# Local attention on Trainium2: where the softmax's division is done

## What is computed

```python
def local_attention(q, k, v):              # 8 heads of 64, windows of 128 tokens
    bq = q.reshape(b, h, w, WINDOW, d) * QK_SCALE
    bk, bv = (look_around(bk), look_around(bv))   # the window before and the own one: 256 keys
    sim = jnp.einsum('bhwid,bhwjd->bhwij', bq, bk)
    mask = (i < j) | (i > j + WINDOW) | (j == -1)
    sim = jnp.where(mask, -jnp.finfo(sim.dtype).max, sim)
    attn = jax.nn.softmax(sim, axis=-1)
    out = jnp.einsum('bhwij,bhwjd->bhwid', attn, bv)

def _layer(x, wqkv, qs, ksc, wo, ...):
    qkv = shift_token(x) @ wqkv
    q = l2norm(q) * qs; k = l2norm(k) * ksc
    q, k = rotary_xpos(q, k)
    x = x + local_attention(q, k, v) @ wo
    ...                                     # then a gated feed-forward
```

## Time and profile before

| | |
|---|---|
| median of 3 runs | 3619.47 us (3614.95 to 3624.1) |
| the profiled execution, its own time | 3632.49 us |
| its span, first to last instruction | 3630.7 us |
| mean granted TensorE clock over the span | 0.947 |
| local attention, layer 0, first to last score matmul | about 772 to 1241 us of the span |
| local attention, layer 1 | about 1537 to 2001 us |
| TensorE busy over the whole span | 3202.5 us (88%) |
| VectorE busy | 2445.3 us (67%) |
| ScalarE busy | 1847.3 us (51%) |

### The profile page before, as it was taken

One profiled execution on the slowest core, in us unless ns is written; L12 is line 12 of the kernel. 1 busy time (PEld: TensorE's weight loads), 2 busy tenths in 40 slices (PEclk: granted clock), 3 DMA queues, 4 the chain that ended last, 5 costly groups with the idle time before them and its releaser, 6 DMA issues. The chain is left out here.

```text
span 3630.7 us, 52188 instructions
## 1 busy us (share of the span) xinstructions
PE 3202.5 (88%) x18048; PEld 1973.5 (54%) x18048; DVE 2445.3 (67%) x4613; ACT 1847.3 (51%) x3942; POOL 1410.3 (39%) x968
## 2 busy tenths in 40 slices
PE   8499999979999799899999899798388888887867
PEld 5244444346666555566666555333255555555756
DVE  8488887657777622277777332498599999997623
ACT  2177776846666421166666211365377777774100
POOL 4201111132222211132222211243599999996522
PEclk9699999989999899999999999899699999999888
DMA  5945666110020043000200121343525151512874
GB/s 171 157 58 89 85 91 125 34 35 23 23 65 23 26 156 97 26 23 23 65 23 19 55 70 47 97 159 141 222 77 204 58 204 58 203 58 73 280 232 153
DMA packets 276034, 347.27 MB, mean 96 GB/s; under 512 B 70619, under 2 KB 207817, under 8 KB 275132
## 3 DMA queue, kind: packets, MB, share of 16 engines
q1 hardware_dynamic: 261860, 308.29, 30.7%
q10 hardware_dynamic: 9432, 23.35, 2.0%
q0 software_dynamic: 4480, 12.30, 0.9%
HBM read 227.72 MB, written 112.80 MB: 94 GB/s over the span
## 5 line engine op out<-in xcount | busy, mean ns | idle before, releaser
L2373 POOL TENSOR_TENSOR H_feed<-H_ndu,H_bs 128x1024 f32<-128x1024 f32 x256 | 595.2, 2369 | 6.6 <-DMA H_cs<-between_bc 4.0
L888 ACT ACTIVATE B_probs<-B_p_exp,B_key_bias 128x512 f32<-128x512 f32 (+3 forms) x768 | 394.7, 582 | 168.0 <-PE B_p_exp L950 137.1
L779 DVE TENSOR_REDUCE B_part_max<-B_p_max 128x1 f32<-128x512 f32 (+3 forms) x768 | 374.7, 546 | 86.8 <-PE B_p_max L914 84.2
L1298 ACT ACTIVATE D_probs<-D_scores,D_neg,D_rq 128x256 f32<-128x256 f32 x512 | 282.9, 574 | 255.5 <-DVE D_neg L1219 255.5
L2344 ACT ACTIVATE H_decay<-H_ndt,H_rate 128x1024 f32<-128x1024 f32 x256 | 287.8, 1125 | 197.5 <-DVE H_turning L2426 102.9
L1658 PE MATMUL E_p_ag<-E_hT,FA_w 128*128 128x512 f32 x640 | 283.6, 603 | 1.9 <-ACT E_hT L1614 1.9
L911 PE MATMUL B_p_max<-B_k,B_q 100*128 100x512 bf16 (+3 forms) x768 | 257.4, 341 | 30.4 <-DMA B_q<-in_q_rows 20.8
L947 PE MATMUL B_p_exp<-B_q,B_k 100*128 100x512 bf16 (+3 forms) x768 | 250.8, 330 | 27.6 <-DMA B_q<-B_shift_rows 20.9
L2426 DVE TENSOR_TENSOR_SCAN H_turning<-H_decay,H_feed 128x1024 f32<-128x1024 f32 x112 | 253.5, 2274 | 24.2 <-POOL H_feed L2373 21.6
L2477 PEld LDWEIGHTS H_p_y<-H_minus,H_sT 128*128 128x128 f32 x1792 | 225.1, 200 | 75.6 <-ACT H_sT L2329 55.9
L2477 PE MATMUL H_p_y<-H_minus,H_sT 128*128 128x128 f32 x1792 | 233.7, 287 | 35.7 <-ACT H_sT L2329 35.7
(11 more groups left out here) (275 smaller groups left out, 6794.0 us busy)
## 6 DMA issues: line engine op xcount, KB each, us to landing
H_bs<-between_bc SPq DMA_DIRECT2D x64, 512.0 KB, 7.7
H_cs<-between_bc SPq DMA_DIRECT2D x36, 512.0 KB, 8.4
B_q<-between_q_parts SPq DMA_DIRECT2D x90, 128.0 KB
B_k<-between_k_parts SPq DMA_DIRECT2D x90, 128.0 KB
between_slots_x<-E_clear ACTq DMA_DIRECT2D x4, 2570.0 KB, 18.7
I_xe<-between_slots_x ACTq DMA_DIRECT2D x32, 257.0 KB, 3.0
LA_base<-between_z SPq DMA_DIRECT2D x64, 128.0 KB, 2.1
between_z<-D_z SPq DMA_DIRECT2D x64, 128.0 KB
```

Of the source, the lines that this page charges most:

```text
L779: nc.vector.reduce_max(part_max[:, g % 2, kc, qb, h:h + 1], p_max[:, use % 3, 0:keys], AX.X).then_inc(maxed, 1)
L888: nc.scalar.activation(probs[:, x % PROBS, skip:512], p_exp[:, n % SCORES, skip:512], ACT.Exp, bias=key_bias[:, g % SETS, kb - 4 * Q + 4, ...
L1298: last = nc.scalar.activation(probs[:, place[m], :, :].rearrange("p a b -> p (a b)"), scores[:, place[m], :, :].rearrange("p a b -> p (a b ...
L2373: nc.gpsimd.tensor_tensor(feed[:, n % AHEAD, :], ndu[:, g % 2, :], bs[:, s, :], ALU.mult).then_inc(fed, 1)
```

## The change

VectorE divides the probabilities by their sums before TensorE turns them, four heads at a time. A new `divide(i, n)` takes, after the exponentials of half n, the reciprocal of four sums and multiplies 128 x 1024 probabilities in place; `turn_p` waits for that (`normal`) and not for `exped`. `invert`, `spread_inv`, `put_invT` and the old `divide` go, with their tiles. The result of `weigh` is copied to SBUF by ScalarE (`put_yT`), behind `put_v`. On TensorE, `project_v` and `turn_h` now stand ahead of `turn_p(i, 0)`. On VectorE, `divide(i, 0)` stands behind `maxima(i)`, and `divide(i, 1)` behind `rotate` of k. Each head's sum is put at the head's place in `probs`.

```diff
-            def invert(i):
-                dve.wait_ge(exped, 2 * i + 2)
-                nc.vector.reciprocal(inv[:, :], total[:, :]).then_inc(inv_ready, 1)
-                dve.wait_ge(inv_ready, i + 1)
-                reached(dve, inv_spread, i)
-                nc.vector.tensor_copy(inv_wide[:, :, :], inv[:, :].rearrange("p (h a) -> p h a", a=1)
-                                      .broadcast_to([P, LH, LD])).then_inc(wide_ready, 1)
-            def divide(i):
-                dve.wait_ge(weighted, i + 1)
-                dve.wait_ge(invT_ready, i + 1)
-                reached(dve, projected, i)
-                nc.vector.tensor_tensor(yT[:, :, :], p_y.rearrange("p (t q) -> p t q", t=PAIRS), invT[:, :, :], ALU.mult
-                                        ).then_inc(yT_ready, 1)
+            def divide(i, n):
+                half = slice(4 * n, 4 * n + 4)
+                dve.wait_ge(exped, 2 * i + n + 1)
+                nc.vector.reciprocal(inv[:, half], total[:, half]).then_inc(inv_ready, 1)
+                dve.wait_ge(inv_ready, 2 * i + n + 1)
+                heads = probs[:, half, :, :].rearrange("p h s k -> p h (s k)")
+                nc.vector.tensor_tensor(heads, heads, inv[:, half].rearrange("p (h a) -> p h a", a=1)
+                                        .broadcast_to([P, 4, 2 * P]), ALU.mult).then_inc(normal, 1)
...
                 maxima(i)
+                divide(i, 0)
                 if i + 1 < TILES:
                     norms(i + 1, 1)
                     rotate(i + 1, 1)
-                invert(i)
+                divide(i, 1)
                 if i + 1 < TILES:
                     sum_k(i + 1)
                     scale(i + 1)
                     rotate(i + 1, 0)
                     sum_q(i + 1)
-                divide(i)
-                if i + 1 < TILES:
                     norms(i + 1, 0)
...
-            def put_invT(i):
-                act.wait_ge(inv_spread, i + 1)
-                reached(act, yT_ready, i)
-                nc.scalar.copy(invT[:, :, :].rearrange("p t q -> p (t q)"), p_inv).then_inc(invT_ready, 1)
+            def put_yT(i):
+                act.wait_ge(weighted, i + 1)
+                reached(act, projected, i)
+                nc.scalar.copy(yT[:, :, :].rearrange("p t q -> p (t q)"), p_y).then_inc(yT_ready, 1)
...
                 put_pT(i, 1)
-                put_invT(i)
                 if i + 2 < TILES:
                     put_hT(i + 2)
                 if i + 1 < TILES:
                     put_v(i + 1)
+                put_yT(i)
+                if i + 1 < TILES:
                     put_qkT(i + 1)
...
             def turn_p(i, n):
-                pe.wait_ge(exped, 2 * i + n + 1)
+                pe.wait_ge(normal, 2 * i + n + 1)
...
-                turn_p(i, 0)
                 if i + 1 < TILES:
                     project_v(i + 1)
                 if i + 2 < TILES:
                     turn_h(i + 2)
+                turn_p(i, 0)
                 turn_p(i, 1)
-                spread_inv(i)
                 weigh(i, 0)
                 weigh(i, 1)
```

More of the change, by code:

```diff
@@ L1050, in phase_window @@
         inv = a.sb("inv", [P, LH])
-        inv_wide = a.sb("inv_wide", [P, LH, LD])
-        invT = a.sb("invT", [P, PAIRS, P])
         probs = a.sb("probs", [P, LH, 2, P])
@@ L1061, in phase_window @@
         p_y = scores[:, 0:2, :, :].rearrange("p a b c -> p (a b c)")
-        p_inv = scores[:, 2:4, :, :].rearrange("p a b c -> p (a b c)")
         p_h = p_hz[:, 0:KD * P]
@@ L1088, in phase_window @@
         inv_ready = a.sem("inv_ready")
-        wide_ready = a.sem("wide_ready")
-        inv_spread = a.sem("inv_spread")
-        invT_ready = a.sem("invT_ready")
+        normal = a.sem("normal")
         weighted = a.sem("weighted")
@@ L1295, in exps @@
                     reached(act, p_turned, 2 * i)
-                    reached(act, inv_ready, i)
                 for m in range(4 * n, 4 * n + 4):
@@ L1300, in exps @@
                                                 bias=neg[:, m:m + 1], scale=rq[:, i % 2, m:m + 1],
-                                                accum_out=total[:, m:m + 1])
+                                                accum_out=total[:, place[m]:place[m] + 1])
                 last.then_inc(exped, 1)
@@ L1407, in weigh @@
                     last.then_inc(weighted, 1)
[L1409 to L1415, removed]
             def project_z(i):
```

## The result

| | before | after |
|---|---|---|
| median | 3620.93 us (4 runs) | 3755.86 us (4 runs, 3753.62 to 3761.19) |
| ratio | | 1.037, 95% interval 1.0353 to 1.0386 |
| profiled execution, span | 3632.49, 3630.7 us | 3761.19, 3759.4 us |
| undisturbed tile, score to score | 14.87 us | 16.78 us |
| mean of the 62 distances within the two layers | 14.99 us | 17.08 us |

What follows compares the result with a forecast made beforehand. TensorE was taken as the local attention's bound before, a path over the second division after. Path +127, clock +18, stall -2 make +143 us on 3619.5, about 3762 us; range 3728 to 3802.

Steps and rivals of the forecast that it cites:

- The second division on the path: VectorE's second product, queued behind norms and rotate, holds TensorE's second turn 2.19 us; tile 14.87 to 16.86 us.
- The low and the high bound: Price of one 128 x 1024 product on VectorE: 0.70 us low, 1.36 high, 1.225 taken.
- The first division hidden: First product lies under the moved project_v with 0.37 us to spare; without the move TensorE stands 1.6 us a tile.
- The removal, 0.53 us a tile: Four transposes of reciprocals leave TensorE's path; taken alone worth 0.53 us a tile, 34 us in 64 tiles.
- VectorE's freed time: Widening copy (0.43 us) and product on PSUM (0.68 us) leave VectorE; said to cost nothing by themselves.
- What bounds the kernel: In the local attention before the change, TensorE is busy 14.87 of 14.87 us and is the bound; nothing waits.
- The clock: TensorE's standstill in each tile lowers its granted clock at times: 0.29 us a tile, 18 us in all.
- an idle share taken from the scan: Mamba scan, TensorE idle 14% at mean clock 0.98, taken as pattern for 15% idle here.
- The stall at tile 18: A load wait in one local attention tile, 3.4 us with its slow clock; 2 us estimated gained back.
- The port: Second product on VectorE meets GpSimd's power instruction; priced at nothing, or 14 us in all by the skill's lockout.
- the rival of a fall in every tile: TensorE's clock falls in every local attention tile: 83 us in place of 18, 3827 us; chance 9%.

Runs made afterwards that it cites:

- half-product run: Changed kernel with the products taking only the first 128 of each head's 256 keys, so half the probabilities stay undivided; 3678.95 us, ratio 1.0153.
- e12_before_sum_first: Kernel before the change with VectorE's sum_k of the next tile moved ahead of the reciprocals; 3603.37 us, ratio 0.9952.
- e5_weigh_between: Changed kernel with weigh of the first half moved ahead of TensorE's second turn; 3762.34 us, ratio 1.0386.
- e3_yT_first: Changed kernel with ScalarE's put_yT moved ahead of put_v; 3751.75 us, ratio 1.0373.

## Why the prediction held, step by step

The time said was 3762, measured 3755.86; the mechanism is the one predicted.

- **The second division on the path** held. Second turn at 10.53 said, 10.34 measured (889.60 to 899.94); wait 2.19 said, 1.90 measured by the page; tile 16.86 said, 16.78 measured. Two small errors partly cancel in that: the second turn came 0.19 us early, and from it to the next score the path took 6.44 us (899.94 to 906.38) where 6.33 were said. The half-product run shows both products on the path at full price, and the product took the 1225 ns of the earlier trace rows. The low and the high bound for it were not needed.
- **The first division hidden** held, but its price if the cover were gone did not. I said 1.6 us a tile without the move; the run with the move undone has that wait (1.38 us) and the same tile. The second turn waits less by as much. Here a wait ahead of a later wait for the same engine cost nothing.
- **The removal, 0.53 us a tile**, was too much: 0.34 with the division free and the orders mended, and a loss of 0.32 in the change's own orders without the products. Part of those transposes lay in the time in which TensorE would have waited for ScalarE's second copy: with them gone, `weigh` takes 0.30 us longer. And the 0.34 holds 0.42 us by which `turn_qk` and `project_z` got shorter, waits for VectorE for the most part (`e12_before_sum_first` wins 0.29 by VectorE's order alone); so VectorE's freed time, which I priced at nothing, was worth something. None of this is a term of the forecast's sum, where the path over the products takes its place.
- **What bounds the kernel** was read half wrong: "nothing waits" came from modelled ends. `e12_before_sum_first` shows that VectorE's chain set 0.29 us of the tile. For the forecast this did no harm, since the new path is longer than either.
- **The clock** was sized about right: 18 us said; 11 tiles by 1.3 us are 14.5 us. The way to it, an idle share taken from the scan, was right by luck: `e5_weigh_between` keeps the idle share and loses the falls. What counts is that a single standstill is long; how often the clock then falls stays open. The Trainium skill's case ("TensorE: Matmul & The Clock Gate", section "A second HAM failure mode: psum-queue depth-cycling"), a clock that goes back and forth and costs time between bursts, came closest in `e3_yT_first`, where 34 of 60 tiles had it; in the changed kernel 11 of 60 did, not each, and the 3827 of that rival was far off.
- **The stall at tile 18** The earlier trace rows is gone altogether (18.45 to 16.78 for that tile), 3.6 us and not 2.
- **The port** was priced at nothing, and the product did start (898.66) while GpSimd's power ran (897.24 to 898.90), with its usual 1.22 us, so far as GpSimd's spans, which are rough, can show it.

One reading behind the clock was wrong: the trace of the kernel before does have repeated gaps of over 2 us. In its last stage TensorE waits five times, some 21 us apart, for 4.4 to 5.7 us, and the clock fell each time. One gap, and a stretch with it (columns as in the earlier trace rows):

```profile
3517.94 0.66 PE L2990 MATMUL I_bank<-I_ident,I_xr 128*128 128x128 f32 x2 [5.03 <-DMA I_xr<-between_slots_x]
```

```profile
3513.00:3535.00 22.00, 17.06 (x104) 15.56 (x105) 6.50 (x19) 1.55 (x4) 4.33 (x6) 0.84 0.72 218
```

These rows spoke for the rival of a fall in every tile and were left out when it was given 9%; as the gaps are over twice as long as the 1.90 us here, they don't settle it, and the 11 of 60 do.

In sum: 62 x 1.905 = 118.1 us of path (123 for 62 tiles said), 14.5 of clock, 3.6 gained at the stall, and under 1 us net of others give the 129.6 us by which the distances grew.

## What to carry to other kernels

Before moving work off the busiest engine, write out the longest chain through the engine that gets it: here 0.53 us of transposes on TensorE were given up for two products of 1.2 us on a VectorE that was already just in time. A busy share of 100% from modelled matmul ends can hide waits; compare the same group's start-to-start distance in a run where its inputs are early. And when a path gets shorter and the time does not, look at the clock behind the longest standstill: splitting or filling that standstill is worth a try. Here filling it gave 16 us and one split 14, while the other split lost on the path what it gained by the clock.

## What the hardware showed that I had not expected

GpSimd's short instruction behind the power took 0.93 us beside VectorE's product (899.06, the product running from 898.66 to 899.88), against 0.25 for its like at the end of the tile, with VectorE idle. The product itself was not held by GpSimd's power instruction: it started 0.24 us ahead of that one's end. The Trainium skill ("SBUF — State Buffer", section "SBUF: two separate sides") has whichever starts first hold the ports for its whole instruction; here only GpSimd was seen to wait. The short instruction (899.06 to 899.99) agrees with that and the product doesn't, as far as GpSimd's rough spans go. It cost nothing, as `scale` came later still.

Work that is thrown away made a kernel faster: v's projection done twice is 16 us better than done once, at the same undisturbed tile of 16.78 us and without the falls of the clock.
